# Shared experts two batches behind the choice, the first gathers in the experts' block, and results one turn later, in a routed mixture of experts on one core

## What is computed

```python
def _L0_ffn_ref(x, Wg, W1, W2, W3, Ws1, Ws2, Ws3):
    TOP_K = 4
    CAP_FACTOR = 4
    def swiglu(x, w1, w2, w3):
        return jax.nn.silu(x @ w1) * (x @ w3) @ w2
    ...
    scores = jax.nn.softmax(xf @ Wg, axis=-1)
    weights, indices = jax.lax.top_k(scores, TOP_K)
    P = T * TOP_K
    ...
    C = CAP_FACTOR * P // E
    y = jnp.zeros_like(xf)
    for e in range(E):
        pos = jnp.nonzero(pair_expert == e, size=C, fill_value=P)[0]
        ...
        xg = xf[tok]
        out = swiglu(xg, W1[e], W2[e], W3[e]) * w[:, None]
        y = y.at[tok].add(out)
    z = swiglu(xf, Ws1, Ws2, Ws3)
    return (y + z).reshape(B, S, D)
```

## Time and profile before

| | |
|---|---|
| median of 3 runs | 2581.72 us (2581.58 to 2583.26) |
| profiled execution | 2591.22 us, its span 2589.5 us |
| mean granted clock of TensorE | 0.952 |
| the changed stage | 381.1 to 882 us of the span |
| PE, PEld busy | 2254.1 us (87%), 1551.3 us (60%) |
| DVE, ACT, POOL busy | 1368.9 us (53%), 827.8 us (32%), 919.0 us (35%) |
| `xt` gathers (L1627) on POOL | 160, 152.5 us busy, mean 953 ns |

### The profile page before, as it was taken

The page is one execution under the profiler, slowest core; times in us unless marked ns, Lnnn a source line. Parts: engine busy times, 40 slices in busy tenths (PEclk is TensorE's granted clock), DMA queues, the critical chain, the costliest instruction groups (busy, mean ns, idle before and its releaser), DMA issues. The chain is left out here.

```text
span 2589.5 us, 40488 instructions
## 1 busy us (share of the span) xinstructions
PE 2254.1 (87%) x12436; PEld 1551.3 (60%) x12437; DVE 1368.9 (53%) x2986; ACT 827.8 (32%) x1759; POOL 919.0 (35%) x1089
## 2 busy tenths in 40 slices
PE   6999769859888755888888888899999999999997
PEld 3445436558787531333333333656668988889896
DVE  5553355645555555777677775379523333333332
ACT  2222313453233213555565565322211111111111
POOL 1100210265555444455444120122224444444443
PEclk9999979979999877999999999899999999999998
DMA  4000116005555833345433220510038888888885
GB/s 128 0 0 0 44 44 227 28 19 147 144 151 147 151 102 83 82 100 115 95 71 81 67 75 2 181 33 17 17 105 267 260 264 267 261 259 264 270 264 163
DMA packets 188870, 323.19 MB, mean 125 GB/s; under 512 B 29080, under 2 KB 141440, under 8 KB 188779
## 3 DMA queue, kind: packets, MB, share of 16 engines
q1 hardware_dynamic: 148586, 257.68, 30.6%
q0 software_dynamic: 40192, 64.42, 13.2%
HBM read 262.18 MB, written 59.23 MB: 124 GB/s over the span
## 5 line engine op out<-in xcount | busy, mean ns | idle before, releaser
L2695 PE MATMUL me_hp<-me_xgT,me_w 128*128 128x160 f32 x3072 | 434.1, 301 | 3.0 <-DMA me_w<-in_L_ffn_w_exp 1.8
L2695 PEld LDWEIGHTS me_hp<-me_xgT,me_w 128*128 128x128 f32 x3072 | 418.9, 190 | 26.2 <-issue 24.9
L1393 DVE TENSOR_REDUCE hd_nmax<-hd_wide 128x2 f32<-128x1024 f32 x256 | 307.6, 1219 | 129.3 <-PE hd_wide L1131 126.4
L1322 ACT ACTIVATE hd_prob<-hd_slim 128x512 f32<-128x512 f32 x512 | 276.1, 601 | 190.5 <-PE hd_slim L1142 160.9
L2763 DVE TENSOR_TENSOR me_hid<-me_act_out,me_hp 128x160 f32<-128x160 f32 x384 | 123.4, 321 | 334.0 <-ACT me_act_out L2719 299.5
L2719 ACT ACTIVATE me_act_out<-me_hp 128x160 f32<-128x160 f32 x384 | 116.8, 304 | 555.9 <-PE me_hp L2695 443.4
L1142 PE MATMUL hd_slim<-hd_q_stack,hd_k_stack 100*128 100x512 bf16 x512 | 199.5, 393 | 40.5 <-ACT hd_prob L1322 33.7
L1131 PE MATMUL hd_wide<-hd_k_stack,hd_q_stack 97*128 97x512 bf16 x512 | 200.8, 397 | 33.2 <-DVE hd_rest L1387 15.8
L1627 POOL DMA_INDIRECT mr_xt<-routed_rows,mr_token x160 | 152.5, 953 | 151.8 <-DVE mr_e_y L2119 116.0
L2064 PEld LDWEIGHTS mr_e_hp<-mr_e_xtT,mr_e_w_now 128*128 128x128 f32 x1280 | 168.5, 193 | 9.2 <-ACT mr_e_xtT L2084 0.8
L2064 PE MATMUL mr_e_hp<-mr_e_xtT,mr_e_w_now 128*128 128x128 f32 x1280 | 170.1, 276 | 0.0
(11 more groups left out here) (380 smaller groups left out, 3805.8 us busy)
## 6 DMA issues: line engine op xcount, KB each, us to landing
me_w<-in_L_ffn_w_exp SPq DMA_DIRECT2D x192, 512.0 KB
me_w_first<-in_L_ffn_w_exp SPq DMA_DIRECT2D x32, 768.0 KB
me_w_second<-in_L_ffn_w_exp SPq DMA_DIRECT2D x32, 768.0 KB
outputs<-mr_e_y SPq DMA_DIRECT2D x160, 128.0 KB
part_rows<-hd_parts SPq DMA_DIRECT2D x48, 256.0 KB
hd_k_stack<-part_rows SPq DMA_DIRECT2D x192, 64.0 KB
hd_q_stack<-part_rows SPq DMA_DIRECT2D x192, 64.0 KB
mr_w<-in_L_ffn_w_in SPq DMA_DIRECT2D x4, 2048.0 KB, 10.9
```

The costliest lines, as they stand in the source:

```text
L1322: nc.scalar.activation(prob[:, u, :], slim[:, slim_slot(bt, item), :], ACT.Exp, scale=D ** -0.5)\
L1393: nc.vector.tensor_reduce(nmax[:, g % 2, n // 2, c:c + 2], wide[:, at], AX.X, ALU.max, negate=True)\
L2695: last = nc.tensor.matmul(hp[:, f % 3, half * CAP:(half + 1) * CAP], w1[:, sl, c, cols], xgT[:, sl, c, :], start=(c == 0), stop=(c == DC - 1))
```

## The change

- TensorE computes the shared expert of batch b-2 while the choice of batch b is made (`LAG_W` = 2). Its order for a batch becomes: turn(b+1), first(w, 0) twice, `logits(b+1)`, `first(w, 1)` twice, `ranking(b)`, `second(w)`, with w = b-2. `xT` has 4 slots. ScalarE's silus and VectorE's `hiddens` and `add` follow. `logits` no longer waits for `ranked`.
- Batch 6 of the shared expert is computed at the start of the list, batch 7 between the listings of tiles 2 to 9. `add(6)`, the two hiddens of batch 7, `add(7)` and `table_of_tiles` stand among `tiles_of` on VectorE.
- The eight first gathers are issued in the second block, as all the others, no longer at the end of the first. `xt` belongs to the second block and the semaphores of its slots to the whole program. The block's end is what stands between the stored rows and the gathers.
- VectorE's `y` lags by `LAG_O` = 4 tiles, TensorE's `yp` still by 3, the store by 5; `hid` has 4 slots; the table of experts and the register loads are shifted to match. `yp` keeps 2 slots and TensorE's wait before it is unchanged.
- The line that makes the lanes on GpSimd (L1731) is not touched.

```diff
-def mix_experts_routed(nc, ctx, x, ident, stats, mean, rstd, w_gate, w_in, w_out, rows_out, outputs, place, earlier):
+def mix_experts_routed(nc, ctx, x, ident, stats, mean, rstd, w_gate, w_in, w_out, rows_out, x_loaded, outputs, place, earlier):
...
-LAG_H, LAG_Y, LAG_S = 1, 3, 4
+LAG_H, LAG_Y, LAG_O, LAG_S = 1, 3, 4, 5
...
-expert_y = k.sb("expert_y", [1, TILES + UNROLL], I32)
+expert_y = k.sb("expert_y", [1, TILES + 2 * UNROLL], I32)
...
-xt = k.sb("xt", [P, UNROLL, D + E])
...
-x_loaded = [s.sem(f"x_loaded{j}") for j in range(UNROLL)]
-def gather(pool, n):
-    nc.gpsimd.indirect_dma_start(out=xt[:, n % UNROLL, :], out_offset=None, in_=rows_out[:, :],
-                                 in_offset=bass.IndirectOffsetOnAxis(ap=token[:, n:n + 1], axis=0)).then_inc(x_loaded[n % UNROLL], 16)
...
+    LAG_W, X_SLOTS = 2, 4
...
-    xT = k2.sb("xT", [P, 2, DC, S])
+    xT = k2.sb("xT", [P, X_SLOTS, DC, S])
...
-for t, pattern, base, by_row in ((steps_of, [[P, PER]], 0, 0), (tile_no, [[P, 2]], -LAG_Y, 1), (number, [[P, NT]], 0, 1),
+for t, pattern, base, by_row in ((steps_of, [[P, PER]], 0, 0), (tile_no, [[P, 2]], -LAG_O, 1), (number, [[P, NT]], 0, 1),
...
-for sem in stored:
-    pool.wait_ge(sem, 16 * (B // SLOTS))
-pool.wait_ge(tokens_ready, 1)
-for n in range(UNROLL):
-    gather(pool, n)
...
-pe.wait_ge(ranked, b)
...
-    last = nc.tensor.matmul(logit[:, j, :], xT[:, b % 2, c, j * P:(j + 1) * P], wg[:, c, :],
+    last = nc.tensor.matmul(logit[:, j, :], xT[:, b % X_SLOTS, c, j * P:(j + 1) * P], wg[:, c, :],
...
-last = nc.tensor.matmul(hp[:, n, half, :], sw1[:, n, c, half * F:(half + 1) * F], xT[:, b % 2, c, :],
+last = nc.tensor.matmul(hp[:, n, half, :], sw1[:, n, c, half * F:(half + 1) * F], xT[:, b % X_SLOTS, c, :],
...
+    w = b - LAG_W
...
             turn(b + 1, c)
-        first(b, 0, c)
-    ranking(b)
-    for half in range(2):
-        first(b, 1, half)
+        if w >= 0:
+            first(w, 0, c)
...
         logits(b + 1)
-    else:
-        pe.wait_ge(ranked, B)
-        nc.tensor.matmul(counts, ones[:], before[:, TB, :], start=True, stop=True).then_inc(counted, 1)
-    second(b)
-for t in range(NT):
+    if w >= 0:
+        for half in range(2):
+            first(w, 1, half)
+    ranking(b)
+    if w >= 0:
+        second(w)
+pe.wait_ge(ranked, B)
+nc.tensor.matmul(counts, ones[:], before[:, TB, :], start=True, stop=True).then_inc(counted, 1)
+for w in range(B - LAG_W, B - 1):
+    for n in range(NS):
+        for half in range(2):
+            first(w, n, half)
+    second(w)
+def listing(t):
...
+for t in range(NT):
+    listing(t)
+    if 2 <= t < 2 + 2 * NS:
+        first(B - 1, (t - 2) // 2, (t - 2) % 2)
+    if t == 9:
+        second(B - 1)
...
-    nc.scalar.activation(xT[:, b % 2, c, :], tp[:], ACT.Copy).then_inc(xT_ready, 1)
+    nc.scalar.activation(xT[:, b % X_SLOTS, c, :], tp[:], ACT.Copy).then_inc(xT_ready, 1)
+def silu(b, n):
+    act.wait_ge(h_full, b * NS + n + 1)
+    nc.scalar.activation(act_out[:, n, :], hp[:, n, 0, :], ACT.Silu).then_inc(silu_done, 1)
...
+    if b >= LAG_W:
+        for n in range(NS):
+            silu(b - LAG_W, n)
+for b in range(B - LAG_W, B - 1):
...
-        act.wait_ge(h_full, b * NS + n + 1)
-        nc.scalar.activation(act_out[:, n, :], hp[:, n, 0, :], ACT.Silu).then_inc(silu_done, 1)
+        silu(b, n)
...
+if t in (5, 7):
+    silu(B - 1, (t - 5) // 2)
...
-def hiddens(b):
-    for n in range(NS):
-        dve.wait_ge(silu_done, b * NS + n + 1)
-        nc.vector.tensor_tensor(hid[:, n, :], act_out[:, n, :], hp[:, n, 1, :], ALU.mult).then_inc(h_free, 1)
+def hiddens(b, n):
+    dve.wait_ge(silu_done, b * NS + n + 1)
+    nc.vector.tensor_tensor(hid[:, n, :], act_out[:, n, :], hp[:, n, 1, :], ALU.mult).then_inc(h_free, 1)
...
-    if b:
-        add(b - 1)
+    if b > LAG_W:
+        add(b - LAG_W - 1)
...
     ranking(b)
...
-    hiddens(b)
+    if b >= LAG_W:
+        for n in range(NS):
+            hiddens(b - LAG_W, n)
...
-for g in range(NT // GROUP):
-    placing(g)
-    if g == 1:
+for w in range(B - LAG_W, B - 1):
+    add(w - 1)
+    if w == B - LAG_W:
+        placing(0)
+    for n in range(NS):
+        hiddens(w, n)
+for t in range(NT):
+    if t and t % GROUP == 0:
+        placing(t // GROUP)
+    tiles_of(t)
+    if t == 4:
+        add(B - 2)
+    if t in (6, 8):
+        hiddens(B - 1, (t - 6) // 2)
+    if t == 13:
         add(B - 1)
         table_of_tiles()
-    for t in range(g * GROUP, (g + 1) * GROUP):
-        tiles_of(t)
...
+xt = k2.sb("xt", [P, UNROLL, D + E])
...
-hid = k2.sb("hid", [P, 2, P])
+hid = k2.sb("hid", [P, 4, P])
...
-for n in range(UNROLL, TILES):
-    pool.wait_ge(y_ready, n - UNROLL + 1 + 2)
-    gather(pool, n)
+for n in range(TILES):
+    if n >= UNROLL:
+        pool.wait_ge(y_ready, n - UNROLL + 1 + 2)
+    nc.gpsimd.indirect_dma_start(out=xt[:, n % UNROLL, :], out_offset=None, in_=rows_out[:, :],
+                                 in_offset=bass.IndirectOffsetOnAxis(ap=token[:, n:n + 1], axis=0))\
+        .then_inc(x_loaded[n % UNROLL], 16)
...
-nc.tensor.matmul(yp[:, v, 0:D], hid[:, v, :], w2[:, bass.ds(e, 1), :].rearrange("p a n -> p (a n)"),
+nc.tensor.matmul(yp[:, v, 0:D], hid[:, (u - LAG_Y) % 4, :], w2[:, bass.ds(e, 1), :].rearrange("p a n -> p (a n)"),
...
-        pe.load(regs_y, expert_y[0:1, bass.ds(i * UNROLL + UNROLL, UNROLL)])
-pe.load(regs_y, expert_y[0:1, 0:UNROLL])
+        pe.load(regs_y, expert_y[0:1, bass.ds(i * UNROLL + UNROLL + LAG_O - LAG_Y, UNROLL)])
+pe.load(regs_y, expert_y[0:1, LAG_O - LAG_Y:LAG_O - LAG_Y + UNROLL])
...
-regs = [dve.alloc_register(f"expert{u}") for u in range(UNROLL + LAG_Y + AHEAD)]
+regs = [dve.alloc_register(f"expert{u}") for u in range(UNROLL + LAG_O + AHEAD)]
...
-        if not (first and u < LAG_Y) and not (last_ones and u > LAG_Y - 1):
-            v = (u - LAG_Y) % UNROLL
-            dve.wait_ge(yp_full, n - LAG_Y + 1)
-            dve.wait_ge(y_stored[v], i * 16 + (16 if u >= LAG_Y else 0))
+        if not (first and u < LAG_O) and not (last_ones and u > LAG_O - 1):
+            v = (u - LAG_O) % UNROLL
+            dve.wait_ge(yp_full, n - LAG_O + 1)
+            dve.wait_ge(y_stored[v], i * 16 + (16 if u >= LAG_O else 0))
...
-            weights(regs[u + LAG_Y + AHEAD], (u + AHEAD) % W_SLOTS)
+            weights(regs[u + LAG_O + AHEAD], (u + AHEAD) % W_SLOTS)
...
-            nc.vector.tensor_tensor(hid[:, v, :], act_out[:, v, :], hp[:, v, P:2 * P], ALU.mult).then_inc(hid_ready, 1)
-dve.load(regs[0:1], expert_y[0:1, LAG_Y:LAG_Y + 1])
+            nc.vector.tensor_tensor(hid[:, (u - LAG_H) % 4, :], act_out[:, v, :], hp[:, v, P:2 * P], ALU.mult).then_inc(hid_ready, 1)
+dve.load(regs[0:1], expert_y[0:1, LAG_O:LAG_O + 1])
...
+rows_gathered = [k.sem(f"rows_gathered{j}") for j in range(8)]
...
-scratch["routed_rows"], outputs, place, first)
+scratch["routed_rows"], rows_gathered, outputs, place, first)
...
```

## The result

The changed kernel takes 2613.36 us (median of 4 runs, 2605.88 to 2622.98) where the kernel before, run beside it, takes 2582.49 (4 runs, 2581.58 to 2590.50): the ratio is 1.0115 (95% interval 1.0076 to 1.0154), some 30 us slower. The forecast was slower, but with 2592 and an upper end of 2608.

What follows compares the result with a forecast made beforehand. TensorE was taken to bound batches and experts, other engines the list, with the hole open to gain. Batches +10, list +7.5, hole -10 and experts +3 gave +10.5: 2592 us, range 2568 to 2608.

Steps and rivals of the forecast that it cites:

- Batches: First stretch, to the counts: TensorE's waits for hiddens and a lower clock cost +10 us, bounds 0 and +17.
- 1.3 us a pause: Batches: clock loss of 1.3 us for each of four TensorE pauses, bounds 0 and 2.5.
- List: List of tokens: shared-expert work placed there delays listings and `placing(2)`, +7.5 us, bounds +3 and +10.
- F: Start of `first_rows`, at 493.69 us before the change; times in the list are counted from it.
- Hole: TensorE's idle time before the experts: gathers moved past the block's end save 10 us, bounds -9 and -11.
- Experts: Loop of routed experts: effects of the later turn sum to +3 us, bounds -30 and +12.
- Rival D: Experts: double-buffered `yp` decides at every loop end, 12.6 us more, 2604 in all; chance 0.13.
- Late signals: Experts: late TensorE signals; the later turn gains 7 us on `y` waits, loses 10 where `hp`'s signal is late.
- Rival B: Batches: pauses leave the clock whole, batches +3, sum +3.5, 2585 us; chance 0.18.
- C: Experts: gathers spaced by the tile, a tile takes 1.54 us, 2568 in all; chance with Rival E 0.27.
- Rival E: Batches: `second(w)` finds its hiddens ready, 23 us fall away, 2569; chance with C 0.27.
- two rings: Experts: `y(n-2)` before `yp` had 0.7 us of slack; `y`, gather and landing left 1.5 of four tiles' 6.2.

Runs made afterwards that it cites:

- f3: e4 with `second(w-1)` after batch w's first two halves, slots shared and VectorE's hiddens reordered; 1.0010 times the kernel before.
- e4: The changed kernel without its later turn: `y` lags by 3 again, the store by 4, `hid` keeps four slots; 1.0037 times the kernel before.
- f1: The changed kernel as it is, traced on chip 7; 1.0120 times the kernel before, experts 289.9 us.
- g3: f2 with `y`'s factor from a constant tile and gathers waiting only for the transposes eight tiles before; experts came to the expected 262 us.
- e1: The changed kernel with TensorE loading nine registers from a multiple of eight and using the last eight; 1.0112 times the kernel before.
- f2: e1 with four slots of `yp` in place of two; 1.0062 times the kernel before, experts 274.0 us.
- g1: e4 with each gather waiting for the `y` of one tile later; it cost 5.5 us.
- e3: The kernel before with only the eight first gathers moved into the experts' block; 0.9964 times the kernel before.
- f4: The kernel before as it is, traced on chip 7; experts 260.5 us.
- g4: e2 with the table and loads shifted by four places instead of one, VectorE loading 16 registers; experts 265.8 us.
- e2: The kernel before with the table of experts shifted one place, TensorE loading from one word past a multiple of eight; 1.0062 times the kernel before.
- g2: f3 with VectorE's `rows(b+2)` moved ahead of its own ranking step; 0.9943 times the kernel before.

## Why the prediction was wrong

The direction held, the size did not: +10.5 us was forecast, +30 measured, above the range.

- Batches. Right in the sum, +10.3 for +10, and in the mechanism: pause 3.19 for 3.4, a batch 416.69 to 433.58, 16.9 for 17.1. Two parts of it were off and nearly made up for each other, which is luck. Batch 2 began at 401.8, 3.4 us later than the 398.4 I took and past my bound of 400.4: each of batches 0 and 1 took 10.3 us, not 7.5, and in each TensorE waited 2.0 us for VectorE's `rows`, the wait that held f3 later. And the lower clock cost less than 7.2, some 6 us, not evenly (1.3 us a pause) but in single pieces: 2.8 in the `second` shown, 1.7 in the next one, 1.6 at the start of batch 2. No run shows the 1.3 us a pause that the forecast took: the earlier trace rows have 4.6 us at a granted clock of 0.63 after 3.3 us without a matmul, 1.7 us lost, and of the four pauses of 3.19 us one was followed by the loss of 2.8 and three by none. The spread of the batches of one order goes with the clock too: 126.3 to 126.8 us at a mean granted clock of 0.85 (changed kernel, e4, f1, g3), 128.0 at 0.84 (e1), 129.6 at 0.83 (f2, g1).
- List. +4.2 for +7.5, inside its bounds of 3 and 10. `second(7)` began at F + 31.2, as worked out, but `placing(2)` did not wait for the listing of tile 15 and ended at F + 43.7, not 45.8; from there to the tokens it took 33.3 us, 1.4 less than before, at a granted clock of 0.96 in the list where it was 0.84.
- Hole. Right: -10.3 for -10, and e3 shows it alone. From the first gather's issue (582.96 in the changed kernel's trace) to TensorE's first transpose (586.03) are 3.1 us, for the 3.0 taken. The median landing of a gather in the loop, once others run beside it, is 3.7 (f4).
- Experts. Here the sum failed, +16.7 and +29.4 for +3. Three steps of it:
 - "... one more register cost nothing; no row waits for them" spoke for the register loads, and the diff's line that moves TensorE's load by one word was given no price. It costs 10 us alone (g4 to e2), 6 beside the rest (e1 to f1). The register itself is not free either: VectorE's longer load costs 5 us in g4, and with TensorE's ninth register 4 up to tile 144 in g3. The trace of before had the load in it, 0.59 us at each loop end, so that it was worth a look as any other instruction on TensorE's queue.
 - "At the loop's end ... that now delays `y(n-2)`, against a slack of 0.7" named the right place and then gave it nothing in the sum. It costs 10 us (f2 to e1), 13 up to tile 144. Rival D had this mechanism, at 12.6 us and a chance of 0.13; for it the size was about right and the weight too low.
 - "... of four tiles' 6.2 us, y, gather and landing take 4.6, and 1.5 is left" fits a tile in the middle of the loop. At a loop end `y` comes 3.2 us after its `yp`, not 1.4, and the gather is left 3.4 us for a landing of 3.5. Near the end of the stage landings of 7.2 us take the place of the 3.0 I took. That is 12.9 us (g3 to f2), 4.5 of them in the first 144 tiles and the rest in the last 16.
- Late signals. I put the turn's gain at -7 for the short stretch and a loss of 10 for the long one. In the first pair the waits before `yp` shrank by 17.6 us in all. That this is the later turn's gain is not shown, since TensorE now also stands for 30 us before its transposes, in which the other engines catch up. On chip 7 there is hardly a wait for a hidden in either kernel (0.5 and 1.5 us in front of `yp`), and the loss stands bare at 29. What makes the signals late stays open; no later run shows it, and spacing the gathers was not tried.
- Rival B (no clock loss) and C (tiles at 1.54) did not come. Rival E, that the second layer finds its hiddens ready, came true in f3 and g2, where VectorE's order was changed too, and paid only in g2.

## What to carry to other kernels

When work is put a step later in a software pipeline, go round every ring that it belongs to (the slots of its input, of its output, and the buffers beside it) with the times of the loop's end, not of its middle: two rings here had 0.7 and 1.5 us of room by my own working, and one was overdrawn at every loop end (21 waits of `yp` in e1), the other at some of them and in the last 16 tiles. Treat a queue's register load as an instruction with a price (0.59 to 2.35 us on TensorE's queue here), and look at the word on which it begins when a table is shifted. And a change that moves work of one engine has to be followed in the order of the engine that feeds it: the same lag of two batches cost 10 us of the batches' time in one order and saved 15 in another. With the work that went into the list counted it cost 14 and saved 7. Last, an experiment that lands on the expected total has not yet shown the mechanism: g3 did so with 4 us too much in one part and 5 too little in another.

## What the runs showed of the hardware

- The time of a register load went with where it began, not only with how many words it had: on TensorE's queue eight words took 0.59 us from a multiple of eight, 0.60 from four past it (g4), 2.10 (e2) to 2.35 us (first trace of the changed kernel) from one past it; nine words from a multiple of eight 0.85 to 1.02. On VectorE's, all from a multiple of eight, 12 words took 0.88 to 1.00, 13 took 1.09 to 1.19 and 16 took 1.18. All are medians of a trace. What rule lies behind it is open.
- A pause of TensorE of one length did not always cost its clock: in the changed kernel's trace three of four pauses of 3.19 us were followed by a `second` of 3.72 us and one by a `second` of 6.56, and of two pauses of 1.90 one by 5.41 and one by 3.72.
- The landing of a gather went with where in the stage it lay: in f2 it took a median of 3.5 us up to tile 144 and 7.2 after it, with the DMA engines busy for 0.60 and 0.84 of the time.
- The same kernel took 2582 us in the first measurement and 2541 to 2543 on chips 7 and 10, and 38.5 of these 41 us lie in one loop of 160 tiles (299.0 and 260.5 us). That the first ran on another chip is likely and not on record. Who tunes a loop by the waits of one trace may be tuning that chip.
